# One reciprocal for a head's four row sums, the scalings of the probabilities shared by ScalarE and VectorE, and new step orders

## The reference

```python
scale, shift = jnp.split(emb @ W_emb + b_emb, 2, axis=-1)
xn = _rms_norm(x, g_norm) * (1.0 + scale) + shift
q, k, v = xn @ W_qkv                      # as 16 heads of 64
q = _rms_norm(q, g_q); k = _rms_norm(k, g_k)
logits = jnp.einsum('bhqd,bhkd->bhqk', q, k) * d ** (-0.5)
attn = jax.nn.softmax(logits, axis=-1)
o = jnp.einsum('bhqk,bhkd->bhqd', attn, v)
x = x + o + o @ W_out
```

## Time and profile before

| | |
|---|---|
| three runs | 2258.46, 2259.87, 2263.42 us |
| median | 2259.87 us |
| span of the profiled execution | 2255.9 us |
| PE busy, of the span | 2176.2 us, 96% |
| PEld busy | 1992.2 us, 88% |
| DVE busy | 1748.6 us, 78% |
| ACT busy | 1411.7 us, 63% |
| POOL busy | 931.4 us, 41% |

### The profile page before, as it was taken

How to read it: one execution, slowest core, us unless ns; L and a number is a source line. 1 busy time by engine, 2 the same in 40 slices (tenths; PEclk the granted TensorE clock), 3 DMA queues, 4 the chain that set the end, 5 groups by cost and what they waited for, 6 DMA issues and landing times.

```text
span 2255.9 us, 39472 instructions
## 1 busy us (share of the span) xinstructions
PE 2176.2 (96%) x13392; PEld 1992.2 (88%) x13392; DVE 1748.6 (78%) x3511; ACT 1411.7 (63%) x3077; POOL 931.4 (41%) x1241
## 2 busy tenths in 40 slices
PE   7788789999999999999999999999999999999999
PEld 3676678999999999999999999999999999999989
DVE  4799988678985699767986689857897569876786
ACT  4577766467854577546864578646775458754663
POOL 3866674235532345223541246312553325422330
PEclk9899999999999999999999999999999999999999
DMA  7655464777556765568555675566654775656842
GB/s 299 238 212 226 188 224 147 269 269 254 192 187 241 271 218 196 175 236 289 207 202 197 230 285 192 189 238 242 230 205 165 254 281 199 203 192 227 294 157 103
DMA packets 141528, 497.55 MB, mean 221 GB/s; under 512 B 14864, under 2 KB 61968, under 8 KB 140304
## 3 DMA queue, kind: packets, MB, share of 16 engines
q1 hardware_dynamic: 141328, 495.03, 61.7%
HBM read 425.77 MB, written 69.21 MB: 219 GB/s over the span
## 4 chain that ended last, share of the span: by engine, by line
PE 77%; DVE 11%; issue 4%; DMA 4%; ACT 3%; POOL 1%; SPq 0%; DVEq 0%; ACTq 0%
PE proj_bank L597 16%; PE proj_bank L599 16%; PE proj_bank L598 16%; PE flip_bank L721 8%; PE pv_bank L732 5%; PE pv_bank L733 5%; PE score_bank L713 4%; PE score_bank L714 4%; DMA w_ring<-qkv_store 2%; DVE neg_max L1069 2%; DVE probs L1075 2%; PE score_bank L686 2%; DVE pt_lo L1079 1%; ACT pt_hi L866 1%; ACT probs L860 1%
## 5 line engine op out<-in xcount | busy, mean ns | idle before, releaser
L597 PE MATMUL proj_bank<-w_ring,xa_hi 128*128 128x384 f32 x1792 | 626.5, 350 | 21.0 <-DVE xa_lo L1058 7.6
L599 PE MATMUL proj_bank<-w_ring,xa_lo 128*128 128x384 f32 x1792 | 606.4, 338 | 0.0
L598 PE MATMUL proj_bank<-w_ring,xa_hi 128*128 128x384 f32 x1792 | 605.7, 338 | 0.0
L860 ACT ACTIVATE probs<-score_bank,neg_max 128x512 f32<-128x512 f32 x512 | 352.1, 690 | 250.0 <-DVE neg_max L1069 242.6
L866 ACT CAST pt_hi<-flip_bank 128x512 fp32r<-128x512 f32 x512 | 296.3, 586 | 235.7 <-PE flip_bank L721 148.3
L1079 DVE TENSOR_TENSOR pt_lo<-flip_bank,pt_hi 128x512 fp32r<-128x512 f32 x512 | 346.6, 686 | 117.0 <-ACT pt_hi L866 111.6
L1069 DVE TENSOR_REDUCE neg_max<-score_bank 128x1 f32<-128x512 f32 x512 | 341.4, 684 | 75.0 <-PE score_bank L714 71.7
L597 PEld LDWEIGHTS proj_bank<-w_ring,xa_hi 128*128 128x128 f32 x1792 | 340.6, 190 | 40.8 <-issue 13.5
L598 PEld LDWEIGHTS proj_bank<-w_ring,xa_hi 128*128 128x128 f32 x1792 | 341.3, 190 | 9.6
L599 PEld LDWEIGHTS proj_bank<-w_ring,xa_lo 128*128 128x128 f32 x1792 | 339.6, 190 | 0.0
L721 PE MATMUL flip_bank<-ident,probs 128*128 128x128 f32 x2048 | 294.3, 274 | 14.5 <-DVE probs L1075 7.3
(11 more groups left out here) (91 smaller groups left out, 3855.3 us busy)
## 6 DMA issues: line engine op xcount, KB each, us to landing
w_ring<-qkv_store SPq DMA_DIRECT2D x392, 768.0 KB, 5.7
w_ring<-wo_store SPq DMA_DIRECT2D x108, 512.0 KB, 4.7
qkv_store<-w_ring SPq DMA_DIRECT2D x56, 768.0 KB, 4.9
x_tile<-in_x SPq DMA_DIRECT2D x36, 512.0 KB, 7.8
w_raw<-in_x SPq DMA_DIRECT2D x112, 128.0 KB, 6.4
out<-w_raw SPq DMA_DIRECT2D x112, 128.0 KB, 1.9
w_raw<-in_w_qkv SPq DMA_DIRECT2D x16, 768.0 KB, 7.8
wo_store<-w_ring SPq DMA_DIRECT2D x16, 512.0 KB, 5.0
```

Of the source, the lines that this page charges most:

```text
L597: nc.tensor.matmul(dst, a_hi, w[:, 0, :], start=start, stop=False, skip_group_check=shared)
L598: nc.tensor.matmul(dst, a_hi, w[:, 1, :], start=False, stop=False, skip_group_check=shared)
L599: return nc.tensor.matmul(dst, a_lo, w[:, 0, :], start=False, stop=stop, skip_group_check=shared)
L860: nc.scalar.activation(probs[h][:, i, :], score_bank[n % 2][:, :], ACT.Exp, bias=neg_max[:, n:n + 1], accum_out=row_sum[:, n:n + 1]).then_ ...
```

## The change

- `N` is cut in two. A new step `U` on VectorE, two per pair (`U0`, `U1`), takes the reciprocals of a head's four row sums in one instruction on a 128 by 4 tile. It waits for all four exponentials of the head.
- `N` only scales. `N0`, `N1`, `N4`, `N5` stay on VectorE; `N2`, `N3`, `N6`, `N7` go to ScalarE, as an activation `Copy` with the reciprocals as the scale. `F0` and `F4` on TensorE wait for both engines' scalings, through one semaphore each.
- All tables are written anew. They hold the same steps as before, apart from `U` and the `N` that change engine, in another order on all five engines.

```diff
@@ HEAD, "ScalarE", as an example of the tables
-        0L11 0L12 0L13 0D2 0D3 1D0 1D1 0V0 2L0 2L1 0T0 0T1 2L2 0V1 1D2 1D3 0S0 2L3 0S1 0S2 0S3 2E0 2E1 0F0 0F1 0S4 0S5
+        0L9 0L10 0L11 0L12 0D2 0L13 0D3 1D0 2L0 1D1 0T0 0T1 1D2 2L1 0V0 2L2 0S0 0S1 2L3 0S2 0S3 1D3 0N2 0N3 0V1
...
+        probs_ready_act = sem("probs_ready_act")
...
                         if i == 0:
-                            pe.wait_ge(probs_ready, it * 8 + (4 * h + 4))
+                            pe.wait_ge(probs_ready, it * 4 + 2 * (h + 1))
+                            pe.wait_ge(probs_ready_act, it * 4 + 2 * (h + 1))
...
+                    elif kind == "N":
+                        act.wait_ge(inv_done, it * 2 + (h + 1))
+                        nc.scalar.activation(probs[h][:, i, :], probs[h][:, i, :], ACT.Copy,
+                                             scale=row_inv[:, n:n + 1]).then_inc(probs_ready_act, 1)
...
+                    elif kind == "U":
+                        dve.wait_ge(exp_done, it * 8 + (4 * n + 4 + CREDIT))
+                        nc.vector.reciprocal(row_inv[:, 4 * n:4 * n + 4], row_sum[:, 4 * n:4 * n + 4]).then_inc(inv_done, 1)
                     elif kind == "N":
-                        dve.wait_ge(exp_done, it * 8 + (n + 1 + CREDIT))
-                        nc.vector.reciprocal(row_inv[:, n:n + 1], row_sum[:, n:n + 1]).then_inc(inv_done, 1)
-                        dve.wait_ge(inv_done, it * 8 + (n + 1))
+                        dve.wait_ge(inv_done, it * 2 + (h + 1))
                         nc.vector.tensor_scalar(probs[h][:, i, :], probs[h][:, i, :], row_inv[:, n:n + 1], None,
                                                 ALU.mult).then_inc(probs_ready, 1)
```

More of the change, by code:

```diff
@@ L75 @@
-    "VectorE": """
[L76 to L96, removed]
@@ new lines @@
+    "SyncE": """
+        0H0 0H1 0H2 0H3 0H4 0H5 0H6 0H7 0H8 0H9 0H10 2G0 2G1 2G2 0H11 0H12 +X0 2G3 0H13 2H0 2H1 2H2 +X1 2H3 2H4
+        2H5 2H6 2H7 2H8 2H9 2H10 4G0 4G1 4G2 2H11 2H12 4G3 2H13 4H0 +X2 4H1 4H2 4H3 4H4 +X3 4H5 4H6 4H7 4H8 4H9
+        4H10 6G0 6G1 6G2 4H11 4H12 6G3 4H13 6H0 6H1 6H2 6H3 6H4 6H5 6H6 6H7 6H8 6H9 6H10 G0 G1 6H11 6H12 8W0
+        6H13 8W1 8W2 8W3 8W4 8W5 8W6 8W7 8W8 E0 8W9 8W10 8W11 8W12 8W13 H0 G4 H1 E1 H2 G5 O0 E2 O1 H3 E3 E4 E5
+        H4 O2 E6 G8 H5 H6 G9 O3 H7 10W0 E7 10W1 10W2 O4 10W3 10W4 O5 10W5 O6 10W6 E8 10W7 10W8 E9 10W9 10W10
+        10W11 10W12 10W13 E10 H8 O7 G12 H9 H10 E11 G13 H11 H12 H13 H14 O8 O9 12W0 O10 O11 E12 E13 12W1 O12 E14
+        H15 E15 O13 12W2 O14 12W3""".split(),
@@ L165 @@
[L165 to L169 removed]
+        4C0 4C1 4C2 2W0 2W1 4C3 4C4 2F4 2W2 2W3 4C5 2F5 2W4 2F6 4C6 2F7 4C7 4C8 2W5 2W6 3F0 3S6 3S7 3F1 2W7 4C9
@@ new lines @@
+    "GpSimd": """
+        0Q0 3V0 +A0 1Q0 3V1 4D0 4M0 +A1 +A2 4D1 4M1 4D2 4M2 2Q0 +A3 4D3 4M3 5D0 5D1 5M0 4V0 5D2 5M1 5M2 5D3 3Q0
+        5M3 4V1 +X0 5V0 5V1 6D0 6M0 6D1 +X7 6M1 +X1 +X8 +X4 +X11 6D2 6M2 6D3 6M3 +X5 7D0 7M0 +X10 4Q0 7D1 6V0
+        7D2 7M1 7M2 6V1 7D3 7M3 +X3 +X9 +X12 +X2 5Q0 7V0 7V1 8D0 8M0 +X6 8D1 8M1 8D2 8M2 6Q0 8D3 8M3 +X13 9D0
+        7Q0 9D1 8V0 9M0 9D2 9M1 9D3 9M2 8V1 9M3 10D0 9V0 9V1 10D1 10M0 10M1 10D2 10M2 10D3 10M3 11D0 11D1 10V0
+        11M0 11M1 11D2 11M2 11D3 11M3 10V1""".split(),
@@ new lines @@
+    "SyncE": """
+        +X0 4W4 +X1 -O15 4W5 +X2 +X3 4W6 4W7 4W8 4W9 4W10 4W11 4W12 4W13 6W0 6W1 6W2 6W3 6W4 6W5 6W6 6W7 E0 E1
+        6W8 6W9 6W10 6W11 6W12 E2 6W13 8W0 8W1 8W2 E3 8W3 8W4 8W5 8W6 E4 8W7 E5 8W8 E6 E7 8W9 E8 8W10 E9 8W11
+        8W12 8W13 W0 W1 W2 W3 W4 O0 W5 O1 W6 W7 10W0 O2 10W1 10W2 O3 10W3 10W4 O4 10W5 E10 E11 10W6 O5 O6 10W7
+        O7 10W8 10W9 10W10 10W11 10W12 10W13 W8 W9 E12 W10 W11 O8 W12 W13 O9 W14 O10 W15 12W0 E13 E14 12W1 O11
+        E15 O12 12W2 O13 12W3 O14""".split(),
@@ L199 @@
     "GpSimd": """
-        0Q0 1Q0 3V0 3V1 4D0 2Q0 4D1 4D2 4D3 4M0 4M1 4M2 4M3 4V0 4V1 5D0 5M0 5D1 5D2 5M1 5M2 5D3 5M3 3Q0 5V0 6D0 5V1 6D1
-        6M0 6M1 6D2 4Q0 6M2 6D3 6M3 7D0 7M0 5Q0 7D1 7D2 6V0 7M1 7M2 7D3 7M3 6V1 7V0 7V1 6Q0 7Q0""".split(),
+        0Q0 3V0 1Q0 4D0 4M0 3V1 4D1 4D2 4M1 4D3 4M2 4M3 4V0 5D0 2Q0 5M0 5D1 5D2 5M1 4V1 5M2 5D3 5M3 6D0 5V0 6M0
+        3Q0 6D1 6M1 5V1 6D2 4Q0 6D3 6M2 6M3 5Q0 6V0 7D0 7D1 7M0 6V1 7D2 7M1 7M2 7D3 7M3 7V0 7V1 6Q0 7Q0""".split(),
     "SyncE": """
-        E0 E1 E2 -O15 E3 4W4 4W5 4W6 4W7 4W8 4W9 4W10 4W11 4W12 4W13 6W0 6W1 6W2 6W3 6W4 6W5 6W6 6W7 6W8 6W9 6W10 6W11
@@ L204 @@
-        6W12 6W13 W0 W1 W2 W4 W5 W6 W8 W9 W10 W12 W13 W14 W3 W7 W11 W15 O0 O1 O2 O3 O4 O5 O6 O7 O8 O9 O10 O11 O12 O13
-        O14 O15""".split(),
+        4W4 4W5 4W6 4W7 4W8 4W9 4W10 4W11 4W12 4W13 6W0 6W1 6W2 6W3 6W4 6W5 6W6 6W7 6W8 6W9 E0 6W10 E1 6W11 6W12
+        6W13 W0 E2 W1 W2 E3 W4 W5 -O15 W6 W8 W9 W10 W12 W13 W14 W3 W7 W11 O0 O1 O2 W15 O3 O4 O5 O6 O7 O8 O9 O10
+        O11 O12 O13 O14 O15""".split(),
 }
```

260 lines of the change are left out of this document (138 added, 122 removed).

## The result

The changed kernel takes 2211.61 us (2210.67 to 2211.8, 4 runs), the kernel before 2260.48 us (2258.46 to 2263.42, 4 runs): 49 us less, a ratio of 0.9783 with a 95% interval of 0.9769 to 0.9797. The prediction had the sign and the region, but 2240 us and a range down to 2217: the gain was more than twice what was forecast.

What follows compares the result with a forecast made beforehand. VectorE was taken to bound the first 395 us and TensorE the rest. Relief of VectorE, 15.1 us, plus 5 us behind 395 us made 20 us less, so 2240 us, with a range of 2217 to 2257 us.

Steps and rivals of the forecast that it cites:

- What bounds the kernel: Whole kernel: VectorE bounds the first 395 us, TensorE the rest; five VectorE waits early sum to 36.5 us.
- The relief of VectorE, 15.1 us: First 395 us: 31.7 us leave VectorE, 8.5 come back, net 23.2; 65% on the path gives 15.1 us.
- The share of 65%: First 395 us: 30.8 of 47.6 us of VectorE's scalings lie on the chain that ended last.
- The wait at `U`: First 395 us: VectorE waits for a head's last exponential, 0.5 us a head, 8.5 us for 17 heads.
- It is part of the 15.1 and not added.: First transposition, early stretch: its 7.3 us wait for scaled probabilities shrinks, with no gain counted beyond VectorE's relief.
- The count of steps: Steady batches: 11.8 TensorE steps between score and transposition, up from 8.9; 7.5 between `F` and `W`, up from 6.4.
- ScalarE's price: Scalings moved to ScalarE: 0.68 us each, between a cast at 0.62 and the exponential at 0.69.
- ScalarE near to a bound at 80%: First 395 us: 23 us more bring ScalarE to 80% busy, VectorE to 84%, so not all 31.7 us count.
- Behind 395 us, 5 us: Behind 395 us: a third of TensorE's 14 us of idle time comes off, 5 us.
- the last rival: Score loop: ScalarE's scalings delay exponentials and TensorE waits; 45 heads hit give 2271 us; chance 0.11.
- The signs: Profile after: VectorE's early busy time falls 25 to 32 us, steady batches begin 13 to 18 us earlier.
- The larger gain: Whole kernel: all 31.7 us of VectorE's relief and all 14 idle us behind 395 us go, 2214 us; chance 0.15.

Runs made afterwards that it cites:

- order_head: Kernel before, with the changed kernel's tables for batch 0 alone on all five engines and the old instructions everywhere: 2237.41 us, 0.9910.
- new_head: Changed kernel's table and instructions for batch 0, those of the kernel before from there on: 2220.42 us, 0.9824.
- after_load: Changed kernel, with each of VectorE's 32 scalings in batch 0 done twice: 2226.66 us, 0.9864.
- relief_all: Kernel before, with all 64 scalings and their reciprocals left out in batch 0: 2238.58 us, 0.9910.
- relief_before: Kernel before, with 32 of 64 scalings left out in batch 0 and the reciprocals kept: 2246.54 us, 0.9949.
- order_only: Changed kernel's tables throughout, with the old instructions, all scalings and reciprocals on VectorE: 2299.11 us, 1.0188 to the kernel before.
- ops_only: Tables of the kernel before, with one reciprocal a head and half of the scalings on ScalarE: 2377.73 us, 1.0534.
- after_no_act: Changed kernel, with ScalarE's 32 scalings in batch 0 left out: 2210.54 us, 0.9784 to the kernel before.
- head_start: Kernel before, with only the steps ahead of batch 0's first score in the new order: 2251.1 us, 0.9957.
- warm: Kernel before, with transpositions that nobody reads put into TensorE's long waits in batch 0: 2259.33 us, 0.9996.
- warm_more: As warm, with nearly twice the unread transpositions at the same places: 2261.07 us, 1.0009 to the kernel before.

## Why the prediction was right and wrong

The changed kernel came out below the stated range. By the ratios the 49 us fall apart in three steps of runs: the new order of batch 0 with the old instructions, 20 us (order_head, 0.9910); the new instructions in that order, 19 us (new_head, 0.9824); the later batches, 9 us (the changed kernel, 0.9783). The intervals leave 6 to 7 us of play on the first two and 4 on the last. The traces, read at the 94th score, divide the 41 us of batch 0 into 25.0 for the order and 16.1 for the instructions (464.54 in order_head, 448.48 in new_head).

- *What bounds the kernel.* Right in the main. 41.5 of 47.0 us were won in batch 0's table, VectorE's entries in the list of waits shrank from 36.5 to under 7 us, and after_load shows that time added to VectorE counts there. But 13.6 us of those entries (`xa_lo`, and nearly all of the transposition's wait for `pt_lo`) went by the order, with VectorE's load unchanged (order_head), so that they named VectorE did not make them a matter of its load.
- *The relief of VectorE, 15.1 us.* The size is near, 16 to 19, but partly by luck. The share of 65%, read from the chain, is too high in the old order (0.4 in relief_all; 0.51 in relief_before, which leaves it open) and too low in the new one (15 to 18 us for 18.2 added). The wait at `U` was priced at 8.5 us for the stretch; VectorE's idle time before the reciprocal between 69 and 395 us was

```profile
DVE row_inv L1092 <- ACT probs L875: 4.9, 10, 1.1
```

- *"It is part of the 15.1 and not added."* This is the step that failed. I took the new tables as cover for one wait, that for scaled probabilities (7.3 us before, 0.8 after), and the sum has no term for the new order in batch 0. It was worth 20 us by the runs and 25 by the trace, a quarter to a half of it at the start. Even the one wait was not covered by the order: with the old instructions it is 8.0 us (order_head), and it went with the relief. The trace before had a part of what the order won: a wait of 7.6 us on VectorE's `xa_lo`, where no scaling stands, and 4.6 us on GpSimd's beside it. I used the sum of the list only to show that VectorE binds, and did not ask which entries the new order removes without any relief. How the order's gain behind the start divides between shorter waits and the clock stays open.
- *The count of steps.* More steps between a score and its transposition, and between an `F` and its `W`, were read as less waiting. In the changed kernel the two waits that these counts speak of, for scaled probabilities and at the products with v for `pt_lo`, are indeed shorter in batch 0, but order_head has the same steps and does not wait less at either. That the tables would be bad for the old instructions, and the old tables for the new ones (order_only, ops_only), was not foreseen, and does not show in either trace.
- *ScalarE's price.* The scaling takes 724 ns in the median, above both of my bounds, 619 and 690. The estimate by the Trainium skill ("ScalarE: Activation LUTs", What ACT_TABLE_LOAD costs), 0.71 us, was nearer. It changed nothing: the whole of it costs nothing measurable in batch 0 (after_no_act). The reciprocal of four columns takes 177 ns, not 154.
- *ScalarE near to a bound at 80%.* Wrong: it is at 82%, nearly level with VectorE, and without its scalings the time is the same. A high share did not make it the bound.
- *Behind 395 us, 5 us.* Near: 5.5 by the traces behind the 94th score, 9 with the seam by the runs. PEld's waits there changed in kind, against the earlier trace rows:

```profile
PEld pv_bank L747 <- DVE pt_lo L1099: 7.5, 20, 1.0
PEld score_bank L727 <- ACT probs L875: 6.5, 24, 0.4
PEld flip_bank L736 <- DVE pt_lo L1099: 4.7, 10, 0.9
PEld flip_bank L736 <- issue: 3.9, 14, 0.7
```

That for the exponential halved (12.8 to 6.5), which the last rival had feared to grow; those for `pt_lo` doubled (6.1 to 12.2, of which 0.3 to 4.7 ahead of the transposition).

- *The signs.* As said: TensorE's waits for scaled probabilities are 0.8 and 0.2 us, the mean of VectorE's scalings in the early stretch is 0.598 us, its idle time ahead of a reciprocal is 0.29 us a head (37.6 / 128), and what lies behind the 94th score shortens by 5.5. Not as said: the steady batches begin 41 us earlier, not 13 to 18; and VectorE's busy time in the first 395 us falls by 13.9 us (322.6 to 308.7), not 25 to 32, since more of the work was done within them.
- *The larger gain* (2214 us) named the right size by a wrong mechanism: full relief and no idle time behind. The mean granted clock did rise, from 0.989 to 0.997 of the span. That is 24.8 us' worth of clock lost before (2255.9 x 0.011) and 6.6 after, so by this estimate at most 18 us of the 47 can be the clock's. Almost all of it goes with the order: by the means over all executions order_head rises from 0.988 to 0.995, up to 15 of its 20 us, and head_start from 0.988 to 0.992, up to 7 of its 10, while new_head has 0.996, which leaves about 1 of the instructions' 19 us to the clock. Whether the clock is a cause or only follows the shorter gaps stays open, since warm and warm_more hardly moved it; clock and order cannot be parted by these runs.

## What to carry to other kernels

When a change brings new tables of steps and new instructions, price them apart: go through the list of waits and ask of each entry whether the new order removes it without any change of load. A share of the chain is not a price: the same engine's microsecond was worth 0.4 to 0.5 in one order and 0.8 to 1 in the other. And a table and its instructions can need each other: over the whole kernel the tables alone were slower by 41 us and the instructions alone, as I placed them, by 120, both together faster by 49. It need not hold for every stretch: in batch 0 the new order was faster with the old instructions too.

## What the runs showed of the hardware

- An activation `Copy` with a scale operand, 128 by 512 float32 within SBUF, took 724 ns in the median on ScalarE, more than the exponential out of PSUM (690).
- A reciprocal of 4 columns took 177 ns and one of 1 column 154.
- VectorE's scaling within SBUF took 479 to 487 ns in the median and up to 1483 ns before and 1597 after; its mean between 69 and 395 us, where GpSimd is busier than behind it (65% against 37% before), was 700 before and 598 after. No run here isolates why.
